# A fused attention block: early 32-query blocks swapped for five products per row tile, and another order of the start

## The reference, cut to what matters

```python
xn = layernorm(x, g_in)                                   # x: 64 x 128 x 512
q = (xn @ Wq).reshape(b, n, H, DH).transpose(0, 2, 1, 3) * scale
kv = xn @ Wkv
k, v = kv[..., :DH], kv[..., DH:]
k = concatenate([nk, k], axis=1); v = concatenate([nv, v], axis=1)
sim = einsum('bhid,bjd->bhij', q, k) + bias               # bias: 16 x 128 x 129, shared by all sequences
sim = where(causal_mask, neg, sim); sim = where(mask, sim, neg)
attn = softmax(sim)
out = einsum('bhij,bjd->bhid', attn, v).transpose(0, 2, 1, 3).reshape(b, n, INNER)
return x + layernorm(out @ Wo, g_out)
```

## Time and profile before

| what | us |
|---|---|
| runs, median of 3 | 1069.54, 1069.09, 1062.03: 1069.09 |
| the profiled execution | 1064.88 |
| its span | 1063.0 |
| PE busy | 1029.5 (97% of the span) |
| POOL busy | 828.9 (78%) |
| DVE busy | 765.8 (72%) |
| ACT busy | 661.2 (62%) |

### The profile page before, as it was taken

One profiled execution on the slowest core, in us unless ns is written; L12 is line 12 of the kernel. 1 busy time (PEld: TensorE's weight loads), 2 busy tenths in 40 slices (PEclk: granted clock), 3 DMA queues, 4 the chain that ended last, 5 costly groups with the idle time before them and its releaser, 6 DMA issues.

```text
span 1063.0 us, 42980 instructions
## 1 busy us (share of the span) xinstructions
PE 1029.5 (97%) x14254; PEld 902.9 (85%) x14254; DVE 765.8 (72%) x3513; ACT 661.2 (62%) x2620; POOL 828.9 (78%) x1488
## 2 busy tenths in 40 slices
PE   6789999999999999999999999999999999999986
PEld 6678898888888888888888888888888889889875
DVE  4777777777777777786777787776777777777663
ACT  5655675666675665675665676565676565666552
POOL 2867887778878778878778788788788778787775
PEclk8999999999999999999999999999999999999998
DMA  7312222232222222222223122223222223121101
GB/s 213 124 34 86 77 81 89 67 94 76 63 85 82 74 87 73 68 84 85 76 82 91 50 87 84 86 70 89 62 78 85 83 73 93 54 84 59 50 25 60
DMA packets 90013, 84.01 MB, mean 79 GB/s; under 512 B 21568, under 2 KB 64064, under 8 KB 89792
## 3 DMA queue, kind: packets, MB, share of 16 engines
q1 hardware_dynamic: 88336, 81.03, 25.3%
q10 hardware_dynamic: 1456, 0.04, 0.1%
HBM read 40.11 MB, written 16.78 MB: 54 GB/s over the span
## 4 chain that ended last, share of the span: by engine, by line
PE 89%; issue 2%; POOL 2%; ACT 2%; DVE 1%; POOLq 0%; DVEq 0%; ACTq 0%
PE ps_proj L500 38%; PE ps_pv L488 33%; PE ps_s L452 9%; PE ps_pv L477 9%; ACT exp_bot L914 1%; POOL w_nrm L1112 1%; ACT exp_top L914 1%; POOL y_out L1156 0%; POOL y_nrm L1152 0%; DVE logit_bot L608 0%; DVE o_lo L630 0%; POOL bias_b L1103 0%; ACT xn L942 0%; POOL small L1138 0%; DVE wt L624 0%
## 5 line engine op out<-in xcount | busy, mean ns | idle before, releaser
L914 ACT ACTIVATE exp_bot<-logit_bot,neg_max 128x129 f32<-128x129 f32 x512 | 201.6, 399 | 252.0 <-DVE neg_max L608 223.0
L1103 POOL TENSOR_TENSOR bias_b<-bias_c,mask_add 128x256 f32<-128x256 f32 (+1 forms) x512 | 291.9, 599 | 45.3 <-DVE neg_max L608 45.2
L500 PE MATMUL ps_proj<-xt_hi,wq_hi 128*128 128x256 f32 x1024 | 302.5, 295 | 7.5 <-DVE q_sb L690 6.0
L500 PE MATMUL ps_proj<-xt_lo,wq_hi 128*128 128x256 f32 x1024 | 288.6, 282 | 0.9 <-issue 0.9
L500 PE MATMUL ps_proj<-xt_hi,wq_lo 128*128 128x256 f32 x1024 | 288.6, 282 | 0.0
L608 DVE CUSTOM_DVE_ANT_0 logit_bot<-ps_s,bias_b 128x128 f32<-128x128 f32 x512 | 128.3, 288 | 180.1 <-PE ps_s L452 162.4
L500 PEld LDWEIGHTS ps_proj<-xt_hi,wq_hi 128*128 128x128 f32 x1024 | 193.3, 189 | 24.9 <-issue 13.0
L1112 POOL TENSOR_TENSOR w_nrm<-exp_bot,w_inv 128x256 f32<-128x256 f32 x256 | 156.9, 613 | 65.2 <-DVE w_inv L617 65.2
L488 PE MATMUL ps_pv<-wo_hi,o_hi 128*128 128x512 f32 x488 | 199.0, 408 | 1.2 <-DVE o_lo L630 1.2
L488 PE MATMUL ps_pv<-wo_lo,o_hi 128*128 128x512 f32 x488 | 193.5, 397 | 0.0
L500 PEld LDWEIGHTS ps_proj<-xt_hi,wq_lo 128*128 128x128 f32 x1024 | 193.4, 189 | 0.0
(11 more groups left out here) (94 smaller groups left out, 1778.6 us busy)
## 6 DMA issues: line engine op xcount, KB each, us to landing
x_in<-in_x_dram SPq DMA_DIRECT2D x32, 512.0 KB, 4.1
x_res<-in_x_dram SPq DMA_DIRECT2D x64, 256.0 KB, 2.9
out_dram<-y_out SPq DMA_DIRECT2D x64, 256.0 KB, 2.1
x_split<-xn SPq DMA_DIRECT2D x480, 32.0 KB, 1.9
v_rep<-v_raw SPq DMA_DIRECT2D x256, 32.0 KB, 1.9
w_raw<-in_L_cond_Wq_dram SPq DMA_DIRECT2D x4, 512.0 KB, 11.7
w_raw<-in_L_cond_Wo_dram SPq DMA_DIRECT2D x4, 512.0 KB, 5.2
mask_u<-in_mask_BxS_bk_dram SPq DMA_DIRECT2D x31, 32.0 KB, 3.7
```

Source lines behind the costliest of these rows:

```text
L500: mm = pe.matmul(ps[:, 0:TOK], w[:, k, cols], xt[:, slot, k], start=(j == 0), stop=(j == len(todo) - 1))
L914: ins = nc.scalar.activation(out_[:, s, j], in_[:, s, j], ACT.Exp, bias=neg_max[:, s, k:k + 1], scale=-1.0, accum_out=w_sum[:, s, k:k + 1])
L1103: ins = nc.gpsimd.tensor_tensor(out_, bias, key_mask, ALU.add)
```

## The change

**Queries and keys.** The first two 32-token blocks of every sequence trade places everywhere in the core (PLACED): in `x_split`, in the columns that PE's turn writes (now a product with a permuted identity, `placing`, in place of a transpose), in the bias and mask. Then row tiles 0 and 2 have three late and two early products, tiles 1 and 3 four late and one early: five each, 40 as before. Since `y_out` and `x_res` now hold the rows in the swapped order, each store and each load of `x_res` is made of three DMAs of 32, 32 and 64 rows (PIECES).

**The start.** The late half of the bias is issued from ACT's queue into a raw buffer, the early half from SP between the second and third quarter of Wq; POOL makes the bias of each `c` in five instructions out of it (two of them swap blocks), and takes over the high half of the second quarter of Wq. The null bias comes in one contiguous DMA, and DVE rearranges it. ACT loads its table early and waits for fewer columns. PE warms up with 50 products and 10 more behind the turn. The lists of all engines stand in another order up to the eighth step.

```diff
-WARM = 30
+WARM = 50
+WARM_X = 10
+PLACED = (1, 0, 2, 3)
 ITEMS = (
-    [(1, 0), (1, 1), (1, 2), (0, 0)],
-    [(1, 0), (1, 1), (1, 2), (1, 3), (0, 0), (0, 1)],
+    [(1, 0), (1, 1), (1, 2), (0, 0), (0, 1)],
+    [(1, 0), (1, 1), (1, 2), (1, 3), (0, 1)],
 )
...
+        def placed(rows):
+            return ((rows[0:BLK], slice(BLK, HALF)), (rows[BLK:HALF], slice(0, BLK)), (rows[HALF:N], slice(HALF, N)))
...
             def load_res(q, i):
-                sp.dma_start(x_res[:, i % GB], x_pairs[q, :, i, :]).then_inc(ld_res[i % GB], 16)
+                for rows, at in placed(x_pairs[q, :, i, :]):
+                    sp.dma_start(x_res[at, i % GB], rows).then_inc(ld_res[i % GB], 16)
...
-                        sp.dma_start(x_split[BLK * r:BLK * (r + 1), :, a],
+                        sp.dma_start(x_split[BLK * r:BLK * (r + 1), :, PLACED[a]],
...
-                sp.dma_start(out_pairs[p + back // (2 * GB), :, back % (2 * GB), :], y_out[:, b]).then_inc(stored[b], 16)
+                for rows, at in placed(out_pairs[p + back // (2 * GB), :, back % (2 * GB), :]):
+                    sp.dma_start(rows, y_out[at, b]).then_inc(stored[b], 16)
...
-                nc.vector.tensor_scalar(mask_add[:, k], mask_u8[:, k], MASKED, -MASKED, ALU.mult,
-                                        ALU.add).then_inc(mask_made, 1)
+                nc.vector.tensor_scalar(mask_add[:, k, :, 0:HALF].rearrange("p b (a j) -> p b a j", j=BLK),
+                                        early_swapped(mask_u8[:, k, :, 0:HALF]), MASKED, -MASKED, ALU.mult, ALU.add)
+                nc.vector.tensor_scalar(mask_add[:, k, :, HALF:N], mask_u8[:, k, :, HALF:N], MASKED, -MASKED,
+                                        ALU.mult, ALU.add).then_inc(mask_made, 1)
...
-                for i in range(1, WP):
-                    wq_high(i)
+                wq_high(2)
+                wq_high(3)
+                x_norm(1, 1)
+                soft(0)
+                q_copies(4)
+                soft(1)
+                q_copies(5)
+                x_high_of(1, True)
+                q_copies(6, 7)
                 wo_high(0)
-                q_copies(4)
-                soft(0)
-                q_copies(5, 6)
-                x_norm(1, 1)
-                q_copies(7)
-                soft(1)
-                wo_high(1)
-                x_high_of(1, True)
-                x_norm(BY_PE, 0)
                 soft(2)
                 front(1, 1, "kv", 0)
                 soft(3)
+                wo_high(1)
+                soft(4)
                 wo_high(2)
-                soft(4)
+                soft(5)
+                x_norm(BY_PE, 0)
+                soft(6)
                 wo_high(3)
-                soft(5)
-                soft(6)
                 soft(7)
```

More of the change, by code:

```diff
@@ L313, in front_parts, with load_bias_late, load_bias_early @@
                 yield 2 * p + t // CG + ahead, (t // CG + ahead) % 2, kind, i
+        by_head = attn_bias.rearrange("(c u e) i j -> u e i c j", u=2, e=2)
+        def load_bias_late(eng, u, e):
+            eng.dma_start(bias_raw[HALF * u:HALF * (u + 1), :, N * e:N * (e + 1)],
+                          by_head[u, e, HALF:N]).then_inc(ld_bias, 16)
+        def load_bias_early(eng, u, e):
+            for a in range(2):
+                row = HALF * u + BLK * PLACED[a]
+                eng.dma_start(bias_raw[row:row + BLK, :, BOT + HALF * e:BOT + HALF * (e + 1)],
+                              by_head[u, e, BLK * a:BLK * (a + 1), :, 0:HALF]).then_inc(ld_bias, 16)
         block = ctx.enter_context(nc.Block())
@@ L504, in front @@
                 ps = bank_of(slot, kind, i)
[L505 to L517, removed]
+                by_pe = isinstance(f, int) and f == 0
+                if kind == "kv":
+                    wait(pe, q_made, QT * f - 1)
                     wait(pe, xt_lo_made, XT * (f + 1))
@@ L541, in first_group @@
                 scores(0, 0)
-                for i in range(4, QT):
-                    front(0, 0, "q", i)
+                front(0, 0, "q", 4)
+                front(0, 0, "q", 5)
+                turn_x(1)
+                front(0, 0, "q", 6)
+                front(0, 0, "q", 7)
                 scores(0, 2)
-                for i in range(XT):
-                    front(1, 1, "x", i)
                 front(1, 1, "kv", 0)
@@ L707, in _ @@
             mask_of(0, 0)
+            dve.wait_ge(ld_rows, 16)
+            for u in range(2):
+                up = slice(HALF * u, HALF * (u + 1))
+                nc.vector.tensor_copy(nb_row[up], nb_all[up].rearrange("p (c u e) -> p u c e", u=2, e=2)[:, u]).then_inc(nb_made, 1)
             def wq_low(i):
-                dve.wait_ge(wq_hi_made, KT * (i + 1))
+                if i == 1:
+                    dve.wait_ge(wq_hi_by_pool, KT)
+                else:
+                    dve.wait_ge(wq_hi_made, KT * (1 if i == 0 else i))
                 for k in range(KT):
@@ L969, in _ @@
             act.dma_start(gin_col[:], g_in.rearrange("(k p) -> p k", p=P),
-                          allow_slow_non_contiguous=True).then_inc(ld_cols, 16)
+                          allow_slow_non_contiguous=True).then_inc(ld_gin, 16)
+            act.wait_ge(filled, 1)
+            nc.scalar.copy(y_shift[:], eps_col[:]).then_inc(table_loaded, 1)
+            for u in range(2):
+                for e in range(2):
+                    load_bias_late(act, u, e)
+            act.dma_start(nb_all[:], null_bias.partition_broadcast(P)).then_inc(ld_rows, 16)
             act.dma_start(nk_col[:], null_kv[0].rearrange("(d o) -> d o", o=1)).then_inc(ld_cols, 16)
@@ L1171, in _ @@
             pool.wait_ge(causal_made, 2)
+            nc.gpsimd.memset(causal_early[:], 0.0).then_inc(early_zero, 1)
+            pool.wait_ge(early_zero, 1)
+            for u in range(2):
+                row = HALF * u + BLK
+                nc.gpsimd.memset(causal_early[row:row + BLK, 0:BLK], -MASKED).then_inc(early_filled, 1)
+            pool.wait_ge(early_filled, 2)
+            for g in range(P // BLK):
+                row, h = BLK * g, g % 2
+                own = causal_early[row:row + BLK, BLK * h:BLK * (h + 1)]
+                nc.gpsimd.affine_select(out=own, in_=own, compare_op=ALU.is_ge, fill=-MASKED, base=0,
+                                        pattern=[[-1, BLK]], channel_multiplier=1).then_inc(early_filled, 1)
```

161 lines of the change are left out of this document (105 added, 56 removed).

## The result

| kernel | us, median (range) | against before, 95% interval |
|---|---|---|
| before | 1067.8 (1062.0 to 1069.5) | |
| changed | 1119.8 (1111.4 to 1122.8) | 1.0484 (1.0414 to 1.0554) |

What follows compares the result with a forecast made beforehand. PE, on 89% of the chain, was taken as the bound. Terms -4.5 + 3 - 1.2 + 0.7 = -2.0 against 1064.9 gave 1062.9; predicted 1064 us, range 1049 to 1092 (1056 to 1072 for the forecast case alone).

Steps and rivals of the forecast that it cites:

- The start: Loads and lists ahead of the first output projection: about 1.2 us gained, at 60.8; bounds +2 and -3, or -9.
- PE's 30 additional warming products: Start of PE's list: they lie in time in which PE waits anyway; nothing in the sum.
- the price of an issue on SP: Stores and `x_res` loads: fewer partitions not dearer, so eight more issues at 0.56 us cost 4.5 us a group.
- Value blocks: PE's value products: a block 0.14 us shorter, reaching the output projection in 32 blocks, -4.5 us, between 0 and 8.3.
- the prediction's rule on independent tiles: Value blocks: only the tile with the most products counts; saving at the upper end, 0.26 us a block.
- SP's pieces: Split stores and `x_res` loads delay `x_in`; PE loses 0.2 us in 15 narrow groups, +3 us, between 0 and 9.
- rival 1: SP comes too late: pieces at 0.84 us each, 7.8 us more per group, giving 1132; halfway price 1086; chance 0.22.
- ACT's two rows: Loads ACT issued at the start: 64 partitions in 0.55 us, 128 in 0.60; taken as evidence against rival 1.
- the +2 of my bound: Start: if lists come forward by less, the output projection is later than now, by at most 2 us.
- Tail: Last store at the kernel's end: three issues in place of one, +0.7 us, with nothing behind it.

Runs made afterwards that it cites:

- before_three_pieces: The kernel before with each store and each load of `x_res` in three DMAs of 32, 32 and 64 rows, nothing else; 1086.7 us, ratio 1.0184.

## Why the prediction was wrong

The step that failed most is a sentence in the part on the start: PE's 30 additional warming products "lie in time in which it waits anyway", and the sum has nothing for them. They do run in time in which PE waits, but they are 60 of the 93 instructions by which PE's list ahead of the loop grew, and that growth brought a border to 35 instructions behind the loop's start. Thirty more warming products alone, put into the kernel before, cost 35 us (before_border); 23 further ones in the changed kernel, which moved the border ahead of the loop, gave back 48 us (after_block_start). The second step that failed is the price of an issue on SP.

The sum of what was measured: pause +45 to +48 (by the ratios and by the medians), pieces +17 to +22, tiles in SBUF -13, values -3.5, and some +1 to +3 for the start, gives between +46 and +57; measured +52. The term of the start was not measured apart: it is what the first output projection came later. The prediction's terms one by one:

- **Value blocks, -4.5 predicted, -3.5 measured.** The mechanism stands: one kind gains, the other nothing. The term's size was off: I took 0.14 us of gain, it is 0.09. The issuing shrank by 0.21, nearly the 0.26 of the prediction's rule on independent tiles (the Trainium skill, "TensorEngine Tiling (Array Packing)", section "Key Properties"), but the last results come only 0.09 sooner: `o_hi` now begins 0.27 us behind PE's next instruction and began 0.15 us behind it before (medians of the two traces, in blocks of this kind). Why was not tried.
- **SP's pieces, +3 predicted, +20 measured.** The price of an issue was mis-sized. Median issues in the changed kernel's trace are 0.34 to 0.44 us for 32 rows, but 0.57 (store) and 0.54 (load) for the 64-row piece; 8 more and dearer ones cost 6.1 us a group, not 4.5, and that passes the point of 5 that rival 1 names. Its value between the two prices, 26 us, is near; the reading of ACT's two rows as a proof that 64 rows cost no more was wrong. The path stands: `x_in`, statistics, copy and PE follow, and in before_three_pieces in every other group only, with 3.2 us for each wait of DVE and 1.4 for each of PE, so some 1.8 absorbed where I had 1.6. In after_block_start, the changed kernel without the pause, DVE waited for x 26 times (43.5 us), so in every group; there that part does not stand.
- **The start, -1.2 predicted, +1.2 to +3.4 seen.** The chain was right: DVE waited 5.69 us for the spread, the first values came at 51.6 (55.75 before), and only the output projection's time was off, 65.51 for 60.8. In the changed kernel the spread was issued from 50.98 on, where I had 46.0: the last exponential of step 5 ended at 49.33 (53.46 before), so the steps of the softmax ahead of it had come forward by 4.1 us and not by 9, and the normalization took the 1.51 us that I had for it. The delay of 3.4 us is above the +2 of my bound.
- **Tail, +0.7 predicted.** From the start of PE's last product to the end of the span it is 6.9 us, 5.9 before: +1.0.
- **At nothing in the prediction: the pause, +45 to +48.** I took it that warming products in waiting time cost nothing. The difference in length of PE's list ahead of the loop, 93 instructions, was to be had from the order of the two programs, and the trace of before shows branches of 3.5 us hidden behind the output projection; I looked at neither. By itself this is nearly as much as the whole slowdown; the pieces' 20 us and the gains from tiles and values nearly cancel. That the sign is rival 1's is thus for the greater part luck.
- **Nor the tiles in SBUF, -13.** Three new tiles were in the diff; I gave them no thought.

## What to carry to other kernels

Where a long unrolled loop runs on an engine, its timing can depend on where its first instruction stands: after any change ahead of the loop, look behind the branch for a wait with no releaser, and shift the loop by some tens of instructions that cost nothing. After any change in the list of tiles compare the mean time of instructions whose shape has not changed; a few unused bytes may be worth more than the change itself. And a queue that waits for long in total has no room for more if the wait stands ahead of the work: load what is urgent before what is merely next, and undo the parts of a change one by one before calling the whole of it a loss: here a change that lost 5% contained a version that gains 1.6%.

## What the runs showed of the hardware

- A border in PE's list of instructions 11, 35 or 68 instructions behind the target of a taken branch cost a pause in every pass, up to 2.6, 2.4 and 2.2 us; 128 instructions behind it, or 11 ahead of it, there was none. Where between 68 and 128 the pause ceases, and how far borders lie from each other, was not tried.
- A packet of 16.4 KB on q8 was over 1.6 to 2.3 us behind the end of such a branch, and PE went on 2.9 to 3.7 us behind it.
- Behind such a pause the granted clock was 0.62 of full over 4.5 us, then 1.00 (changed kernel); in before_border 0.80 over 2.6 us and 0.66 over 3.5, then 1.00.
- Sixty-four bytes in the place of the tiles behind the weights: 113 to 114 against 119 to 120 ns from product to product (128x128 weights, 256 columns, fp32r). 256 or 512 bytes: no difference.
- Issues on SP, medians: 0.35 to 0.43 us for 128 rows of 2 KB between memory and SBUF, 0.34 to 0.44 for 32 of them, 0.54 to 0.57 for 64.
